# Digits between the index searches, and query statistics with the indicator matrix as weights

## The reference

```python
h = DCT(x)                                    # (32, 313, 128)
h = h + softmax(n @ n.T) @ n                  # n = layernorm(h), per clip
q = (n2 @ Wq.T + bq) as 8 heads of 64         # n2 = layernorm(h)
q = layernorm(q) * g + b ; split into halves of 32, each l2-normalised
s0, s1 = halves against 64 keys each          # top 16 of each, with index
cs, ci = all 256 sums of scores and of indices (ix0 + ix1); top 16 by score
w = softmax(scores) ; fi = their indices
h = h + sum_k gelu(n2 . down[fi]) * w * up[fi]
```

## Time and profile before

| | |
|---|---|
| median of three runs | 2086.8 us |
| profiled execution | 2086.99 us, span 2085.2 us |
| granted TensorE clock, mean | 0.770 of full |
| PE busy | 1701.8 us, 82% |
| DVE busy | 1925.5 us, 92% |
| ACT busy | 1217.5 us, 58% |
| POOL busy | 1554.2 us, 75% |

### The profile page before, as it was taken

How to read it: one execution, slowest core, us unless ns; L and a number is a source line. 1 busy time by engine, 2 the same in 40 slices (tenths; PEclk the granted TensorE clock), 3 DMA queues, 4 the chain that set the end, 5 groups by cost and what they waited for, 6 DMA issues and landing times.

```text
span 2085.2 us, 48099 instructions
## 1 busy us (share of the span) xinstructions
PE 1701.8 (82%) x11423; PEld 1296.2 (62%) x11423; DVE 1925.5 (92%) x15878; ACT 1217.5 (58%) x3851; POOL 1554.2 (75%) x2561
## 2 busy tenths in 40 slices
PE   5567888888889898898888898888988989788766
PEld 3335576756767576675667667565765757566556
DVE  3299999999999999999999999999999999999992
ACT  3345656666565566655566665666665556665454
POOL 2238787886878788787878868788787767878765
PEclk9676878768787777877788678876878777787666
DMA  1000000000000000000000000000000000000000
GB/s 35 13 9 2 19 7 8 20 6 19 6 19 7 6 19 9 19 6 18 8 6 19 9 17 9 13 12 6 19 7 19 9 9 16 7 13 9 6 6 11
DMA packets 46672, 24.86 MB, mean 12 GB/s; under 512 B 4955, under 2 KB 46116, under 8 KB 46390
## 3 DMA queue, kind: packets, MB, share of 16 engines
q1 hardware_dynamic: 46390, 21.80, 3.7%
HBM read 11.52 MB, written 10.26 MB: 10 GB/s over the span
## 4 chain that ended last, share of the span: by engine, by line
PE 38%; DVE 30%; ACT 16%; POOL 9%; issue 5%; SPq 0%; another core or an unknown queue 0%; DMA 0%; POOLq 0%; DVEq 0%; ACTq 0%
PE QB L531 8%; DVE alpha L1046 5%; PE FB L449 5%; PE FB L440 4%; PE SC L480 4%; ACT WD L732 4%; DVE idx L1030 4%; DVE idx L1033 4%; DVE hrest L1024 3%; PE QB L519 3%; ACT hi L672 3%; PE FB L421 3%; DVE vals L1028 2%; DVE vals L1021 2%; POOL sa L762 2%
## 5 line engine op out<-in xcount | busy, mean ns | idle before, releaser
L892 POOL TENSOR_TENSOR bw<-beta,wp 128x1024 bf16<-128x1024 bf16 x240 | 508.1, 2148 | 117.2 <-ACT wp L718 117.2
L531 PE MATMUL QB<-bw,alpha 128*128 128x48 bf16 x5120 | 555.0, 278 | 32.2 <-issue 32.2
L531 PEld LDWEIGHTS QB<-bw,alpha 128*128 128x128 bf16 x5120 | 523.1, 151 | 73.9 <-issue 65.5
L732 ACT ACTIVATE WD<-QB 32x96 f32<-32x96 f32 x1280 | 307.7, 240 | 76.4 <-PE QB L531 65.1
L1046 DVE TENSOR_SCALAR alpha<-hi 128x1024 bf16<-128x1024 bf16 x640 | 276.0, 501 | 0.0
L480 PE MATMUL SC<-WK,hidT 128*128 128x512 f32 x320 | 223.2, 787 | 50.6 <-ACT stdT L664 43.7
L1030 DVE FIND_INDEX8 idx<-vals,sraw 128x8 uint32<-128x64 f32 x1280 | 250.9, 219 | 0.0
L1033 DVE FIND_INDEX8 idx<-vals,hrest 128x8 uint32<-128x64 f32 x1280 | 250.7, 220 | 0.0
L1024 DVE MATCH_REPLACE8 hrest<-vals,sraw 128x64 f32<-128x64 f32 x1280 | 249.6, 208 | 0.0
L840 POOL TENSOR_TENSOR ci<-idxf 128x64 f32<-128x64 f32 (+3 forms) x400 | 124.3, 347 | 135.8 <-DVE beta L1052 135.6
L725 ACT ACTIVATE ofin<-QB 128x128 f32<-128x128 f32 x80 | 22.2, 278 | 281.0 <-PE QB L531 278.3
(11 more groups left out here) (205 smaller groups left out, 3963.5 us busy)
## 6 DMA issues: line engine op xcount, KB each, us to landing
res<-h_scratch SPq DMA_DIRECT2D x80, 64.0 KB, 1.8
xin<-in_x SPq DMA_DIRECT2D x32, 128.0 KB
h_scratch<-h2n SPq DMA_DIRECT2D x32, 128.0 KB
out<-ofin SPq DMA_DIRECT2D x64, 64.0 KB, 1.5
h_scratch<-h2n SPq DMA_DIRECT2D x32, 28.5 KB
out<-ofin SPq DMA_DIRECT2D x16, 57.0 KB
xin<-in_x SPq DMA_DIRECT2D x32, 28.0 KB
xin<-in_x SPq DMA_DIRECT2D x32, 0.2 KB
```

What stands on the lines that cost most here:

```text
L531: last = mm(bank[:, 48 * u:48 * u + 48], alpha[:, buf, a, :, 8 * p + u], bwv[:, :, a, :, 8 * p + u], start=(a == 0), stop=(a == 1))
L732: last = A(WD[r, RING[(t - 4) % NT], :, 8 * p:8 * p + 8], blocks[r, :, :, g], ACT.Copy)
L892: last = tt(bw[:, buf, NY * i:NY * i + NY, :], beta[:, buf, :, :], wp[:, buf, i, :].unsqueeze(1).to_broadcast([128, NY, 256]), ALU.mult)
```

## The change

The digit block leaves p = 1 and becomes a function of its own. In a slot with searches it is called between the first and the second index search, otherwise in p = 2; `norms` is called in p = 2 behind it. In ACT's p = 0, `hi` moves behind `idxf`. POOL no longer waits for `beta` ahead of `ci`. In the statistics the indicator matrix (now 40 columns, with `WB` as a fifth chunk) stands as weights and 313 tokens of a clip as data, one group of five matmuls a clip, in (2, 3) and (3, 1); ACT copies each result (40 x 313) to `statT`, and in (3, 2) five PE transposes bring it back to token by statistic.

```diff
-    ["xT0", "hc0", "xnT0", "S00", "S02", "S11", "O0", "hT0", "P00", "P02", "P10", "P12", "VAR", "ST1"],
-    ["xT1", "hc1", "xnT1", "S01", "S10", "S12", "O1", "hT1", "P01", "P03", "P11", "P13", "ST0"],
+    ["xT0", "hc0", "xnT0", "S00", "S02", "S11", "O0", "hT0", "P00", "P02", "VT0", "P10", "P12", "VT1", "ST1"],
+    ["xT1", "hc1", "xnT1", "S01", "S10", "S12", "O1", "hT1", "P01", "P03", "P11", "P13", "VAR", "ST0"],
...
+                if (t, p) in ((2, 3), (3, 1)):
+                    b = t - 2
+                    cols = slice(NF * b, NF * b + NF)
+                    bank = f_claim(pe, f"VT{b}", j)
+                    pe.wait_ge(s["wb_steps"], 9)
+                    for c in range(4):
+                        pe.wait_ge(s["sq_full"], 8 * j + 4 * b + c + 1)
+                        mm(bank[0:40, 0:NF], indc[:, c, :], sq[:, c, cols], start=(c == 0), stop=False)
+                    mm(bank[0:40, 0:NF], indc[:, 4, :], hidTn[:, cols], start=False, stop=True).then_inc(f_full[0], 1)
                 if (t, p) == (3, 2):
                     bank = f_claim(pe, "VAR", j)
-                    pe.wait_ge(s["sq_full"], 8 * j + 8)
-                    pe.wait_ge(s["wb_steps"], 9)
+                    pe.wait_ge(s["vt_full"], 2 * j + 2)
                     for tt in range(NT):
-                        cols = slice(START[tt], START[tt] + 128)
-                        for c in range(4):
-                            mm(bank[:, 40 * tt:40 * tt + 24], sq[:, c, cols], indc[:, c, :], start=(c == 0), stop=(c == 3))
-                        last = mm(bank[:, 40 * tt + 24:40 * tt + 40], hidTn[:, cols], WB[:], start=True, stop=True)
-                    last.then_inc(f_full[0], 1)
+                        last = nc.tensor.transpose(bank[:, 40 * tt:40 * tt + 40], statT[:, START[tt]:START[tt] + 128],
+                                                   ident[0:40, 0:40])
+                    last.then_inc(f_full[1], 1)
...
+                if (t, p) in ((2, 3), (3, 1)):
+                    b = t - 2
+                    bank = f_wait(act, f"VT{b}", j)
+                    after(act, s["stat_full"], j)
+                    A(statT[:, NF * b:NF * b + NF], bank[0:40, 0:NF], ACT.Copy).then_inc(s["vt_full"], 1)
...
-                if p == 0 and exists(k, t, 3):
-                    act.wait_ge(s["eb_full"], n - 2)
-                    after(act, s["alpha_full"], n - 3)
-                    for c in range(NS):
-                        last = A(hi[:, c, :], STE, ACT.Identity, bias=cdig[:, c:c + 1])
-                    last.then_inc(s["his_full"], 1)
...
                     A(idxf[:], idx[:, buf, :, :], ACT.Identity, bias=cquart[:]).then_inc(s["idxf_full"], 1)
+                if p == 0 and exists(k, t, 3):
+                    act.wait_ge(s["eb_full"], n - 2)
+                    after(act, s["alpha_full"], n - 3)
+                    for c in range(NS):
+                        last = A(hi[:, c, :], STE, ACT.Identity, bias=cdig[:, c:c + 1])
+                    last.then_inc(s["his_full"], 1)
...
-                    if exists(k, t, 3):
-                        pool.wait_ge(s["beta_full"], n - 2)
...
+            def digits(k, t):
+                n = NT * k + t
+                if exists(k, t, 3):
+                    old = RING[(t - 3) % NT]
+                    dve.wait_ge(s["his_full"], n - 2)
...
                         for i in range(16):
                             V.max_index(idx[:, buf, i, 0:8], vals[:, buf, i, 0:8], raw[i]).then_inc(chain, 1)
+                        digits(k, t)
                         for i in range(16):
                             dve.wait_ge(chain, 32 + i + 1)
                             last = V.max_index(idx[:, buf, i, 8:16], vals[:, buf, i, 8:16], rest[i])
...
+                if p == 2 and not exists(k, t, 0):
+                    digits(k, t)
+                if p == 2 and t == NT - 1 and exists(k, t, -1):
+                    norms(k + 1)
```

More of the change, by code:

```diff
@@ L55 @@
     READ[f"O{_b}"] = ("h2c_full", 2, _b + 1)
+    READ[f"VT{_b}"] = ("vt_full", 2, _b + 1)
     READ[f"hT{_b}"] = ("hidTn_full", 2, _b + 1)
@@ L99, in build @@
         minusb = sb("minusb", [128, 128], BF16)
-        indc = sb("indc", [128, 4, 24])
+        indc = sb("indc", [128, 5, 40])
         cneg64 = sb("cneg64", [128, 1])
@@ L108, in build @@
         bKs = sb("bKs", [81, 1024], BF16)
-        WB = sb("WB", [128, 16])
+        WB = indc[:, 4, 24:40]
         Bc2 = sb("Bc2", [128, 16])
@@ L139, in build @@
         sq = sb("sq", [128, 4, PT])
+        statT = sb("statT", [40, PT])
         rden = sb("rden", [128, 6])
@@ L244, in build @@
             top_chain cand_chain identb_full wgn_psum wgn_full wk_psum wk_full bk_steps bks_psum bks_full
-            wb_steps stat_full std_steps nrm_steps n2_steps seed4_full""".split()
+            wb_steps stat_full vt_full std_steps nrm_steps n2_steps seed4_full""".split()
         s = {n: sem(n) for n in names}
@@ L304, in _ @@
             loads = [(ident[:], ident_d), (dct[:], dct_d), (sel3[:], sel3_d),
-                     (indc[:], indc_d.rearrange("p (c h) -> p c h", h=24)), (sel[:], sel_d), (row8[:], row8_d),
+                     (indc[:], indc_d.rearrange("p (c h) -> p c h", h=40)), (sel[:], sel_d), (row8[:], row8_d),
                      (gcol[0:64, :], ln_g.unsqueeze(1)), (gcol[64:128, :], ln_g.unsqueeze(1)),
@@ L1003, in norms @@
                 seed(n2[:], xh4[:], y4[:], s["seed4_full"])
+            def digits(k, t):
[3 more added lines that the diff above has]
+                    dve.wait_ge(s["his_full"], n - 2)
+                    after(dve, s["beta_full"], n - 3)
+                    V.scalar_tensor_tensor(out=lo[:], in0=STE, scalar=BASE, in1=hi[:, 0, :], op0=ALU.add, op1=ALU.subtract
+                                           ).then_inc(s["lo_full"], 1)
+                    after(dve, s["quads_full"], 4 * (n - 4))
+                    h8 = hi[:].rearrange("p c (m q) -> p c m q", q=NQ)
+                    a8 = alpha[:, old, :, :, :].rearrange("p a (g c x) q -> p c (a g) x q", g=NG, c=NS)
+                    for xx in range(NX // NS):
+                        last = V.tensor_scalar(a8[:, :, :, xx, :], h8, BASE + float(NY * xx), None, ALU.is_equal)
+                    last.then_inc(s["alpha_full"], 1)
+                    after(dve, s["bw_full"], n - 4)
+                    dve.wait_ge(s["lo_full"], n - 2)
+                    for y in range(NY):
+                        last = V.tensor_scalar(beta[:, old, y, :], lo[:], y - 1.5, None, ALU.is_equal)
+                    last.then_inc(s["beta_full"], 1)
             def slot(k, t, p):
@@ L1034, in slot @@
                             last.then_inc(chain if i < 15 else s["halves_full"], 1)
+                if p == 2 and not exists(k, t, 0):
+                    digits(k, t)
+                if p == 2 and t == NT - 1 and exists(k, t, -1):
+                    norms(k + 1)
                 if p == 1:
[L1036 to L1055, removed]
+                    sums = exists(k, t, 2)
                     if sums:
@@ L1094, in late @@
                     dve.wait_ge(step, 1)
-                    V.tensor_reduce(WB[:], heads(tmpb[:], HALF), AX.X, ALU.add).then_inc(step, 1)
+                    V.tensor_reduce(WB, heads(tmpb[:], HALF), AX.X, ALU.add).then_inc(step, 1)
                     dve.wait_ge(step, 2)
-                    V.tensor_scalar(WB[:], WB[:], 2.0, None, ALU.mult).then_inc(step, 1)
+                    V.tensor_scalar(WB, WB, 2.0, None, ALU.mult).then_inc(step, 1)
                     V.tensor_tensor(heads(tmpb[:]), heads(gbq[:]), bB[:].unsqueeze(1).to_broadcast([128, H, QD]), ALU.mult
@@ L1108, in late @@
                     dve.wait_ge(step, 8)
-                    V.tensor_scalar(indc[:, :, 8:24], indc[:, :, 8:24], gsq[:], None, ALU.mult).then_inc(step, 1)
+                    V.tensor_scalar(indc[:, 0:4, 8:24], indc[:, 0:4, 8:24], gsq[:], None, ALU.mult).then_inc(step, 1)
                 if (t, p) == (1, 0):
@@ L1139, in constants @@
     rows = np.arange(128)
-    indc = np.zeros((128, 4, 24), np.float32)
+    indc = np.zeros((128, 5, 40), np.float32)
     for c in range(4):
@@ L1152, in constants @@
     row8[8] = 1.0
-    return {"ident": np.eye(128, dtype=np.float32), "dct": dct, "indc": indc.reshape(128, 96),
+    return {"ident": np.eye(128, dtype=np.float32), "dct": dct, "indc": indc.reshape(128, 200),
             "sel": sel, "row8": row8, "sel3": sel3.reshape(9, 243)}
```

## The result

The kernel after takes 2177.7 us (median of four runs, 2175.84 to 2180.89), the kernel before 2086.31 beside it: ratio 1.0435 [1.0407, 1.0464], slower. The forecast was 2144. The profiled execution of after took 2178.75 us with a span of 2177.0, so 91.8 us more than the one of before; the forecast had 57.

A forecast was written before the change was run, and what follows sets the result against it. DVE's instruction list was taken to bound the loop, digits and POOL instructions excluding each other; 2087 - 111 (what goes) + 168 (15 pairs x 11.2 us) = 2144 us, range 2105 to 2185, wider range 2035 to 2190.

The forecast's parts named there:

- What goes: Savings on DVE: waits at `v` (16 + 3 us) and `lo` (26), excess in `alpha` and `beta` (66); together 111 us.
- Rival 4: Transposes wait for ACT's copy of the second half, so `v` still waits 16 us: 2160; no chance given.
- The meeting in t = 2: First `alpha` lands inside POOL's `wz`, the next two stand behind `Yw` and `Ye`: 3.2 us a pair (0 to 3.2).
- The wait at `sv`: In t = 2 DVE reaches `sv` before ACT's row sums end: new wait of about 1.4 us a pair (0 to 1.9).
- The other slots: Digits meeting POOL's instructions, a pair: t = 3 0.2 us, t = 4 3.2, t = 0 2.2, t = 1 1.0.
- rival 1: POOL loses the meetings; DVE pays only the 1.4 us wait and short meetings, about 3 us a pair: 2021; chance 0.25.
- rival 2: The excess only changes place: 7.4 us a pair come back, t = 2 paying 4.6, the rest 2.8: 2087; chance 0.13.
- rival 3: POOL becomes the chain, all long ones met in t = 4 and t = 0: 246 us, 2222; chance 0.08.
- The turned statistics at 0: The turned statistics on PE and ACT add 0 to the path (-1.2 to +1 us a pair through `bw`).
- PE's sum of work: Twenty matmuls take 5.2 us for both clips at the higher clock; PE's work stays within 5 us a pair.
- the moved wait of ACT: ACT's wait for the first half, ahead of `zexp`: PE is ahead of DVE, so 0 (to 1.1 us a pair).

The follow-up runs named there:

- experiment 4: The changed kernel with POOL waiting for `beta` again, ahead of `wz`: 2161.96 us, 1.0335 [1.0286, 1.0383] against the kernel before.
- experiment 10: The changed kernel with POOL making `Ye` twice, first into a tile of its own: 2293.85 us, 1.0983 [1.0967, 1.1] against the kernel before.
- experiment 5: The changed kernel with ACT's squares for the second row sums moved from (2, 0) to (1, 3): 2140.48 us, 1.0268 against the kernel before.
- Experiment 3: The changed kernel with `norms` ahead of the digits, after the second maxima of t = 4: 2140.28 us, 1.0246 against the kernel before.
- experiment 1: The kernel before with the turned statistics alone, in the change's places; digits, `hi`, `norms` and POOL's wait as before: 2131.2 us, 1.0206.
- experiment 8: The kernel before with the statistics turned, both halves left in the old place (3, 2): 2075.56 us, 0.9946 [0.9931, 0.9961].
- experiment 6: The changed kernel with `norms` ahead of the digits, POOL waiting for `beta` ahead of `wz`, and ACT's row sums in (1, 3): 2133.54 us, 1.0213.
- experiment 7: The kernel of experiment 6 with the old statistics instead of the turned ones: 2106.18 us, 1.007 [1.0036, 1.0104] against the kernel before.
- experiment 2: The changed kernel with the old statistics, so the digit move alone: 2171.95 us, 1.04 [1.0367, 1.0433] against the kernel before.

## Why the prediction came out as it did

The sign was right, the time lies inside the range, and the forecast was 35 us short. By its steps:

- **What goes** was right in size: `lo` 26 forecast, 27.7 measured; `v` 16 + 3 forecast, 19.0 measured. Not all of it is the waiting that was forecast: 23.7 of `lo` is, and the rest is that `lo` overlaps the instruction ahead of it where it does not wait. And 3.7 us of the 26 stood behind the last search, where such a wait remains. Rival 4 is out.
- **The meeting in t = 2** was right: 3.2 us forecast, 5.79 - 2.76 = 3.0 measured, in all 14 pairs, in the order `wz`, `Yw`, `Ye`. Experiments 4 and 10 show the cause: take POOL out and all of it goes, add one instruction and 1.9 us are added. In experiment 5, without the wait at `sv`, POOL loses here in five of 14 pairs.
- **The wait at `sv`** was mis-sized: 1.4 us a pair forecast, 41.4 / 15 = 2.8 measured, 3.8 to 4.0 in nine pairs. The prediction took ACT's time from the slot of before and only moved DVE. But when t = 0 and t = 1 get shorter (22.4 and 24.3 us), DVE comes sooner and ACT, whose row sums stand behind `hi` and `WD`, does not. Experiment 5 shows the term: the wait goes, and 37 us with it, though other meetings change too.
- **The other slots.** t = 4 was mis-sized, 3.2 for 1.2 + 3.6 = 4.8 us in ten of 14 pairs; that is the bound the prediction gave for POOL not being late. t = 0 was 2.2 for 0 in twelve of 14 pairs, t = 1 was 1.0 for 0.2 or less in eleven of 14 and 1.4 in three, t = 3 was 0.2 for 0. In t = 0 rival 1's pattern holds, POOL loses; as a whole neither it nor rivals 2 and 3 took place, since the excess grew from 66 to 112 us. That excess (640 x 119 ns and 320 x 112 ns) stands against 15 x 9.8 = 147 forecast for the meetings.
- **`norms`** was the step that failed. The diff moves it behind the digits, the prediction says so and gives it no price: it asked only which POOL instructions the digits meet. In the new place `norms` meets `bw` (in four pairs `Yw` and `Ye` too), for 46 us, half of the whole loss. Experiment 3 takes all of that away. The Trainium skill, "SBUF — State Buffer", section "SBUF: two separate sides", counts among the instructions that need the shared ports also those of DVE with two inputs in SBUF, against a GpSimd instruction that reads SBUF; the trace agrees (277 to 1712 ns for `n` from `v` and `n`), and `lo`, one of whose inputs lies in PSUM, keeps its 0.40 us while `wz` runs. The prediction used that section for the digits alone.
- **The turned statistics at 0** failed as a claim about the place. Alone they cost 42 us in the places of the change (experiment 1) and bring 11 in the old one (experiment 8); with the mended digits they cost 27 in the new places (6 against 7). The prediction looked at PE's sum of work and gave the moved wait of ACT "0 (to 1.1 us a pair)"; `lo` alone paid 1.9 a pair (29 / 15). The sum for PE is slightly off as well: four instructions in 1.26 us make 6.3 us for twenty, not 5.2; in after ten of one clip take 2.8, so 5.7 for both.

Measured less forecast, term by term: the digits' meetings -35, `sv` +21, `norms` +46, `zs` +7, together +39, of which the rest of the list takes some back to the 35 that were missing. So that the time came out as near as it did is partly luck: too much for t = 0 and t = 1 stood against nothing for `norms`.

What stays open: the parts don't add up (experiments 2, 4, 6), because whatever shortens one slot changes where POOL and ACT stand in the next. Each single shift is seen in the traces; a sum that would give 91 from the parts is not to be had from these runs. Why POOL takes turns with the digits in t = 4 of before and stands behind them in experiments 1 and 8 is open too.

## What to carry to other kernels

When a block moves, price everything that moves with it, and list for every instruction in the new place which POOL instruction runs there: the cost can be one whole POOL instruction for each that is met, whatever the short one on DVE takes by itself. If POOL is the one that stands, the block pays nothing, but the wait can come back later, as at `n` in experiment 8. Hold the other engines' times for the slots before, too: an engine that gains time arrives earlier at the next meeting, and the wait there can grow by as much. And try the two halves of a change apart: here one half was a gain (0.9946 [0.9931, 0.9961]) that its place and its companion hid.

## What the runs showed of the hardware

- A digit instruction of 418 or 217 ns that stands behind a POOL instruction ends just after it: the third `alpha` of t = 2 takes some 2330 ns beside `Ye`, a `beta` of experiment 10 behind two of them 4235. All of it is shown as busy time of DVE, never as a wait.
- The same slot goes either way. In t = 4 of the kernel after, ten pairs show the alternation above, and four show this:

```profile
690.85 2.76 DVE L1028 TENSOR_SCALAR alpha<-hi 128x1024 bf16<-128x1024 bf16 x8
...
690.16 4.77 POOL L853 TENSOR_TENSOR cs<-vs 128x128 f32<-128x128 f32 x5
```

  One `cs` instruction stands through all twelve digit instructions (3.55 us instead of 0.3), and the digits lose nothing; the slot takes 27.4 us instead of 30.8. But the pairs win little by it: in each of the three steady pairs that follow such a slot, t = 1 takes 27.6 us instead of 24.3, with a new wait of 2.0 us for `zexp` and 1.4 us more than undisturbed in `alpha`. In both cases the record of the POOL instruction begins 0.04 to 0.07 us before the first `alpha`, so the records don't tell the winner from the loser beforehand; what decides such a near tie stays open.
